# One block each for the latent stage and the relative stage of a two-layer decoder on one core

## The chip, the cores and the metric

The kernel runs on one core of a Trainium2 chip. That core has a matrix engine (TensorE, in the rows PE, with its weight loads as PEld), a vector engine (VectorE, DVE), an activation engine (ScalarE, ACT), a general engine (GpSimd, POOL), and SyncE (SP), whose queue issues the DMA transfers. The metric is the device time of one execution in microseconds, from the first to the last work of the core. Lower is better.

## What is computed

`x` has 4 batches of 512 tokens with 128 channels, all fp32. Layer 0 is an RWKV-6 block, a cross attention and a feed-forward with a dense and a sparse path. Layer 1 is a self attention with relative position tables, a cross attention of 16 heads with 64 channels on a context of 32 tokens per batch, and a guided attention in two classes. The two stages of layer 1 that the change touches are these:

```python
    def _L1_attn_ref(x, W_qkv, b_qkv, W_out, b_out, rel_emb_k, rel_emb_v):
        ...
        score = jnp.einsum('bhqd,bhkd->bhqk', q, k) + jnp.einsum('bhqd,qkd->bhqk', q, pe_k)
        attn = jax.nn.softmax(score, axis=-1)
        ctx = jnp.einsum('bhqk,bhkd->bhqd', attn, v) + jnp.einsum('bhqk,qkd->bhqd', attn, pe_v)
        ctx = jnp.transpose(ctx, (0, 2, 1, 3)).reshape(b, s, d)
        return ctx @ W_out + b_out
    def _L1_xattn_ref(latents, context, ln_l_w, ln_l_b, ln_c_w, ln_c_b, Wq, Wkv, Wo, bo):
        ...
        lat = layernorm(latents, ln_l_w, ln_l_b)
        ctx = layernorm(context, ln_c_w, ln_c_b)
        q = (lat @ Wq).reshape(b, n, H, D).transpose(0, 2, 1, 3)
        kv = ctx @ Wkv
        k, v = jnp.split(kv, 2, axis=-1)
        ...
        attn = jnp.einsum('bhnd,bhsd->bhns', q, k) * scale
        attn = jnp.clip(attn, -11.0, 11.0)
        attn = jax.nn.softmax(attn, axis=-1)
        out = jnp.einsum('bhns,bhsd->bhnd', attn, v)
        return out @ Wo + bo
    x = x + _L1_attn_ref(_layernorm(x, axis=-1), ...)
    x = x + _L1_xattn_ref(_layernorm(x, axis=-1), ctx_1024, ...)
```

## The kernel before

The stages run one after another, and each is one or more blocks. A block gives every engine its own program; between two blocks all five engines meet at a barrier. `x` stays in SBUF, channels on partitions. Engines work in the written order, and only semaphores tie them. `g.ps` is PSUM: 8 banks of 128 x 512 fp32. A matmul with a 128-row fp32 weight shows as two instructions, a transpose as one.

`norm_stage` (L138 to L178) is a layer norm in its own block: four centering matmuls (L154), four squares on ACT (L166), four mean matmuls (L158), and per batch an `Ln` and an `Exp` on ACT (L169, L172) and a product on DVE (L178).

**Relative stage.** After its norm comes a projection block (L1346 to L1448): q, k and v for four batches on PE, copies on ACT, the tables `raw` and `rel_v` and the rows `ends` by DMA (L1353, L1358, L1363), and q turned to token order (`swap`, L1396), copied by DVE into `q_tok` and stored to DRAM by SP (L1366). After the barrier the main block begins. SP first loads `qd` from that DRAM scratch (L1772); POOL builds `keys`, `qbd` (L1516) and `qrel` from `qd` (L1525); PE scores (L1552, L1562). There are 64 steps of 32 queries. In each, DVE takes four maxima (L1728), ACT four exponentials (L1695), PE turns four tiles (L1577), DVE copies two of them (L1743) and ACT two (L1684), and PE sums values near the diagonal (L1602) and far from it (L1627). DVE's `picked` (L1734, semaphore `masked`) reads the near sums, and `near_values` of the next step and the three `tail` phases of a batch wait for `masked`. At the end of each batch SP stores `o` in one transfer (L1778), waits for it, and reads it back as `ot` in eight transfers (L1786), which `tail` phase 1 (L1646, L1649) waits for. L1656 is the output product, L1763 the addition to `x`.

**Latent stage.** Two norm stages, of the tokens and of the 128 context columns, are followed by a block of weight products: K and V (L1161), their copies, A = Wq K (L1169, 16 matmuls), U = V Wo (L1178, 64 small ones), with two DVE passes for the affine part (L1199, L1202). The third block is a loop over 16 tiles of 128 tokens: score (L1239), clip in two DVE passes (L1267 from PSUM, L1271 in place), `Exp` (L1298), sum (L1253) and reciprocal (L1255), the product with it on POOL (L1281), four transposes (L1222), a copy on ACT (L1292), and per batch four output matmuls (L1232) and an addition (L1259). `p`, `total` and their PSUM banks have two buffers. PE's order in the loop is score of tile n, turn of tile n-1, and after every fourth tile all four output matmuls of a batch.

## Time and profile before

| | |
|---|---|
| median of 3 runs | 1489.88 us (1484.61 to 1497.74) |
| the profiled execution | 1488.59 us, span of its core 1486.9 us |
| PE busy | 1159.3 us, 78% of the span |
| DVE, ACT, POOL busy | 839.2 (56%), 712.7 (48%), 306.2 us (21%) |
| DMA | 51.61 MB, mean 35 GB/s |
| mean granted PE clock | 0.906 |
| relative stage with its norm | 611 to 1080.4 us |
| latent stage | 1080.4 to 1183 us |

No engine is busy all through, and the chain that ended last reaches back only to the last stage. Since stages are parted by barriers, each is read by itself: when its first and last instructions run, and which wait sets its pace. A line in a timeline merges neighbouring instructions of one kind (x4 is four of them), and the bracket behind it holds the idle time of its engine before it and what ended that.

### The profile page before, as it was taken

The page shows a single profiled execution, that of the slowest core. Times are in us where ns is not written, and L with a number is a line of the kernel's source. Part 1 is how long each engine was busy: PE and PEld are TensorE (multiplying, and loading weights), DVE is VectorE, ACT ScalarE, POOL GpSimd, SP SyncE. Part 2 cuts the span into 40 slices and gives each one's busy share as a digit, 9 for nine tenths or more (in the row PEclk, how much of TensorE's full clock was granted, in tenths as well). Part 3 has the DMA queues.
Part 4 walks back from the last instruction along what each step waited for, and adds up shares of the span by engine and source line. Part 5 has one row for each costly group of instructions (what it writes and reads, how often), then busy time and mean ns, then how long its engine had stood idle before and what let it go on. Part 6 is the DMA issues. An engine that isn't in the chain of part 4 may idle for free. (4 is left out here: it accounts for less than half of the span.)

```text
span 1486.9 us, 35646 instructions
## 1 busy us (share of the span) xinstructions
PE 1159.3 (78%) x14780; PEld 578.3 (39%) x14780; DVE 839.2 (56%) x1359; ACT 712.7 (48%) x1328; POOL 306.2 (21%) x639
## 2 busy tenths in 40 slices
PE   5677677888858997578999999999676655588886
PEld 2222332333233442246666666666443223122221
DVE  3575336777632323237666666666226342799994
ACT  4100443777522223536665665555232332389894
POOL 1443010333202322034223223222002101100000
PEclk9999866999968998689999999999889886699998
DMA  4000006111005320140030030110200000611100
GB/s 163 1 0 0 1 0 213 46 46 46 3 0 115 70 44 0 72 72 4 3 24 4 3 24 3 10 11 3 17 1 0 0 1 1 214 36 47 36 24 30
DMA packets 133665, 51.61 MB, mean 35 GB/s; under 512 B 103113, under 2 KB 125657, under 8 KB 132858
## 3 DMA queue, kind: packets, MB, share of 16 engines
q1 hardware_dynamic: 133506, 49.34, 14.3%
q8 instruction: 118, 1.93, 0.5%
q14 instruction: 41, 0.34, 0.1%
HBM read 33.12 MB, written 15.81 MB: 33 GB/s over the span
## 5 line engine op out<-in xcount | busy, mean ns | idle before, releaser
L1728 DVE TENSOR_REDUCE re_nmax<-ps 128x1 f32<-128x512 f32 x256 | 158.9, 683 | 113.1 <-PE ps L1562 113.1
L1577 PE MATMUL ps<-const,re_p 128*128 128x128 f32 x1024 | 154.8, 284 | 33.0 <-DVE re_pT L1743 26.6
L1695 ACT ACTIVATE re_p<-ps,re_nmax 128x512 f32<-128x512 f32 x256 | 154.5, 693 | 16.2 <-DVE re_nmax L1728 16.2
L850 DVE TENSOR_REDUCE ga_nmax<-ps 128x2 f32<-128x1024 f32 x128 | 147.9, 1217 | 14.3 <-PE ps L656 14.2
L1684 ACT ACTIVATE re_pT<-ps 128x512 f32<-128x512 f32 x128 | 76.6, 598 | 162.0 <-PE ps L1577 162.0
L783 ACT ACTIVATE ga_pt<-ps 128x512 f32<-128x512 f32 x256 | 139.2, 598 | 30.6 <-PE ps L691 28.9
L1577 PEld LDWEIGHTS ps<-const,re_p 128*128 128x128 f32 x1024 | 109.1, 142 | 63.4 <-ACT re_p L1695 47.2
L850 DVE TENSOR_REDUCE da_nmax<-ps 128x2 f32<-128x256 f32 (+3 forms) x128 | 102.3, 822 | 38.3 <-PE ps L667 36.9
L783 ACT ACTIVATE da_pt<-ps 128x512 f32<-128x512 f32 (+3 forms) x256 | 97.5, 438 | 46.6 <-PE ps L691 45.6
L1743 DVE COPY re_pT<-ps 128x512 f32<-128x512 f32 x128 | 82.6, 686 | 22.9 <-PE ps L1577 22.2
L710 PE MATMUL ps<-ga_pt,ga_v 128*9 128x256 f32 x1024 | 81.1, 385 | 9.6 <-ACT ga_osum L796 9.4
L1083 DVE TENSOR_TENSOR ex_u<-ps,ex_s 128x512 f32<-128x512 f32 x48 | 33.2, 692 | 96.6 <-PE ps L1056 96.6
L163 ACT ACT_TABLE_LOAD x8 | 10.3, 1283 | 153.2 <-PEq L298 91.7
L1552 PE MATMUL ps<-re_keys,re_qbd 32*128 32x512 f32 x512 | 74.9, 655 | 5.0 <-POOL re_qbd L1516 5.0
L617 POOL TENSOR_SCALAR_AFFINE_SELECT da_pt<-da_pt 128x256 f32<-128x256 f32 x128 | 52.6, 411 | 126.5 <-ACT da_pt L783 126.5
L1069 ACT ACTIVATE ex_s<-ps 128x512 f32<-128x512 f32 x48 | 28.7, 597 | 93.5 <-PE ps L1056 93.5
L1525 POOL TENSOR_TENSOR re_qrel<-re_qd,const 128x64 f32<-128x64 f32 x256 | 68.6, 300 | 4.8 <-DMA re_qd<-re_q_scratch 4.8
L1512 POOL TENSOR_TENSOR re_keys<-re_k,vec 128x64 f32<-128x64 f32 (+1 forms) x60 | 17.3, 288 | 249.7 <-PE ps L1562 249.7
L1096 POOL TENSOR_TENSOR ex_u<-ex_u,ex_gates 128x512 f32<-128x512 f32 x32 | 40.5, 1265 | 134.1 <-DVE ex_u L1083 70.5
L1627 PE MATMUL ps<-re_pT,re_v_far 128*9 128x128 f32 x1536 | 65.4, 286 | 0.5 <-ACT re_osum L1704 0.5
L656 PE MATMUL ps<-ga_kst,ga_qst 50*128 50x512 bf16 x256 | 52.9, 413 | 12.5 <-DVE ga_nmax L850 9.8
L1056 PE MATMUL ps<-ff_xn,weights 128*128 128x512 f32 x128 | 60.2, 592 | 0.0
(384 smaller groups left out, 2020.9 us busy)
## 6 DMA issues: line engine op xcount, KB each, us to landing
ex_gates<-gates_scratch SPq DMA_DIRECT2D x4, 2048.0 KB, 14.7
da_stacks<-da_qkparts SPq DMA_DIRECT2D x8, 384.0 KB, 3.1
da_qst<-da_stacks SPq DMA_DIRECT2D x32, 96.0 KB, 2.3
da_kst<-da_stacks SPq DMA_DIRECT2D x32, 96.0 KB, 2.4
ga_stacks<-ga_qkparts SPq DMA_DIRECT2D x8, 384.0 KB, 3.1
ga_qst<-ga_stacks SPq DMA_DIRECT2D x32, 96.0 KB
ga_kst<-ga_stacks SPq DMA_DIRECT2D x32, 96.0 KB
da_stacks<-da_qkparts SPq DMA_DIRECT2D x8, 256.0 KB, 3.1
```

Source lines behind the costliest of these rows:

```text
L710: last = nc.tensor.matmul(g.ps[32 * j:32 * j + HD + 1, O_BANK, lo:hi], v9[:, QT * b + kt, 4 * quad + j, :], pt[:, (4 * u + kt) % SLOTS, j, ...
L783: nc.scalar.activation(pt[:, (4 * u + kt) % SLOTS, 2 * pr + par, q0:T], g.ps[:, ST_BANK + (2 * t + par) % ST_BANKS, q0:T], ACT.Exp)\
L850: nc.vector.tensor_reduce(nmax[:, u % 2, :, pr, qt], g.ps[:, score_bank[step]:score_bank[step] + 2, 0:keys_of(qt)], AX.X, ALU.max, negate= ...
L1056: last = nc.tensor.matmul(g.ps[:, 2 * m + n % 2, :], g.w(w)[:, bass.ts(f, 128)], x[:, b, :], start=True, stop=True).then_inc(up, 1)
L1525: nc.gpsimd.tensor_tensor(qrel[:, m, pair, :, :, :, two], qd[:, b % 2, OCT * at:OCT * at + OCT, 4 * pair:4 * pair + 4].unsqueeze(2) .broad ...
L1552: nc.tensor.matmul(g.ps[:, S_BANK + quad, :], qbd[rows, m, :, :, :].rearrange("p o h c -> p (o h c)"), keys[rows, b % 2, m, :], start=True ...
L1577: last = nc.tensor.transpose(g.ps[:, T_BANK + tile % 2, bass.ts(kt, 128)], p[:, QUAD_ORDER[idx], bass.ts(kt, 128)], g.c("ident"))
L1627: last = nc.tensor.matmul(g.ps[32 * j:32 * j + HD + 1, V_BANK, bass.ts(quad, 128)], values, weights, start=kt == 0, stop=kt == QT - 1)
L1684: nc.scalar.activation(pT_of(s, QUAD_ORDER[idx]), turned_of(4 * s + idx), ACT.Identity)\
L1695: nc.scalar.activation(p[:, quad, :], g.ps[:, S_BANK + quad, :], ACT.Exp, bias=nmax[:, s % 2, idx:idx + 1]).then_inc(exped, 1)
L1728: nc.vector.tensor_reduce(nmax[:, s % 2, idx:idx + 1], g.ps[:, S_BANK + quad, :], AX.X, ALU.max, negate=True).then_inc(maxed, 1)
L1743: nc.vector.tensor_copy(pT_of(s, QUAD_ORDER[idx]), turned_of(4 * s + idx))\
```

## The change

In the latent stage the two norms, the weight products and the loop become one block. The context's norm runs in PSUM bank 4 among the token norm's instructions, with its affine part in the scaling; the K and V products follow the four mean matmuls. The additive part of the token norm goes to POOL. The factor 1/8 moves into the copy of A, so that the clip is one DVE pass. `p` and `total` have four buffers; PE turns tile n-2 after the score of tile n and makes one output matmul per tile, seven tiles behind.

```diff
+    NP = 4
+    CN, SC, TU, OUT = 4, 0, 2, 4
+    TURN_LAG, OUT_LAG = 2, 3
...
+                nc.tensor.matmul(g.ps[:, CN, 0:B * LC], g.c("center"), g.ctxT[:, :], start=True, stop=True)\
+                    .then_inc(c_centered, 1)
+                for b in range(B):
+                    nc.tensor.matmul(g.ps[:, b, :], g.c("center"), g.x[:, bass.ts(b, T)], start=True, stop=True)\
+                        .then_inc(centered, 1)
+                    if b == 0:
+                        pe.wait_ge(c_squared, 1)
+                        nc.tensor.matmul(g.ps[:, CN, bass.ts(1, B * LC)], g.c("mean"), csq[:, :], start=True,
+                                         stop=True).then_inc(c_varied, 1)
+                pe.wait_ge(c_normed, 1)
+                for b in range(B):
+                    pe.wait_ge(squared, b + 1)
+                    nc.tensor.matmul(g.ps[:, B + b, :], g.c("mean"), sq[:, b, :], start=True, stop=True)\
+                        .then_inc(varied, 1)
...
+                        if c % 4 == 0:
+                            pe.wait_ge(logged, 2 * side + c // 4 + 1)
...
+                    if n % 4 == 0:
+                        pe.wait_ge(scaled, n // 4 + 1)
...
+                pe.wait_ge(a_copied, 4)
+                for n in range(NTILE + QT + OUT_LAG):
+                    if n < NTILE:
+                        score(n)
+                    if 0 <= n - TURN_LAG < NTILE:
+                        turn(n - TURN_LAG)
+                    if n >= QT + OUT_LAG:
+                        output(*divmod(n - QT - OUT_LAG, QT))
...
+                nc.scalar.activation(csq[:, :], g.ps[:, CN, bass.ts(1, B * LC)], ACT.Ln, bias=g.eps[:, :])\
+                    .then_inc(c_logged, 1)
+                act.wait_ge(c_logged, 1)
+                nc.scalar.activation(csq[:, :], csq[:, :], ACT.Exp, scale=-0.5).then_inc(c_rooted, 1)
+                for b in range(1, B):
+                    act.wait_ge(centered, b + 1)
+                    nc.scalar.activation(sq[:, b, :], g.ps[:, b, :], ACT.Square).then_inc(squared, 1)
+                for b in range(B):
+                    act.wait_ge(varied, b + 1)
+                    nc.scalar.activation(sd[:, b, :], g.ps[:, B + b, :], ACT.Ln, bias=g.eps[:, :]).then_inc(logged, 1)
...
+                                         g.ps[:, n, :].rearrange("p (i n) -> p i n", n=128), ACT.Identity,
+                                         scale=XD ** -0.5).then_inc(a_copied, 1)
...
+                for n in range(NTILE + TURN_LAG):
+                    if n < NTILE:
+                        act.wait_ge(clipped, n + 1)
+                        flat = p[:, n % NP, :, :].rearrange("p h k -> p (h k)")
+                        nc.scalar.activation(flat, flat, ACT.Exp).then_inc(exped, 1)
+                    if n >= TURN_LAG:
+                        copy(n - TURN_LAG)
...
+                    nc.vector.scalar_tensor_tensor(out=lat[:, b, :], in0=g.ps[:, b, :], scalar=g.v("ln_l_w"),
+                                                   in1=sd[:, b, :], op0=ALU.mult, op1=ALU.mult).then_inc(scaled, 1)
...
+                def clip(n):
+                    dve.wait_ge(scored, n + 1)
+                    if n >= NP:
+                        dve.wait_ge(turned, n - NP + 1)
+                    nc.vector.tensor_scalar(p[:, n % NP, :, :].rearrange("p h k -> p (h k)"), g.ps[:, SC + n % 2, :],
+                                            11.0, -11.0, ALU.min, ALU.max).then_inc(clipped, 1)
+
+                def average(n):
+                    dve.wait_ge(exped, n + 1)
+                    if n >= NP:
+                        dve.wait_ge(normed, n - NP + 1)
+                    nc.vector.tensor_reduce(total[:, n % NP, :], p[:, n % NP, :, :], AX.X, ALU.add).then_inc(totalled, 1)
+                    dve.wait_ge(totalled, n + 1)
+                    nc.vector.reciprocal(total[:, n % NP, :], total[:, n % NP, :]).then_inc(inverted, 1)
+
...
+                for n in range(NTILE + QT + OUT_LAG):
+                    if n < NTILE:
+                        clip(n)
+                    if 1 <= n <= NTILE:
+                        average(n - 1)
+                    b, at = divmod(n - OUT_LAG - QT - 1, QT)
+                    if at == QT - 1 and b >= 0:
+                        add(b)
+                add(B - 1)
...
-                    flat = p[:, n % 2, :, :].rearrange("p h k -> p (h k)")
-                    nc.vector.tensor_scalar(flat, flat, -11.0, None, ALU.max).then_inc(floored, 1)
...
+                    pool.wait_ge(scaled, b + 1)
+                    nc.gpsimd.tensor_scalar(lat[:, b, :], lat[:, b, :], g.v("ln_l_b"), None, ALU.add)\
+                        .then_inc(lat_ready, 1)
```

In the relative stage the projections and the steps become one block (the norm stays its own). `xn`, `q_tok`, `zero` and `raw` lie in the second half of `pT`, which is first written in step 4.

```diff
+        pT_all = sb("pT", [128, 2, GS * QT * OCT * QG // 2 * 2 * H])
+        pT = pT_all[:, :, :].rearrange("p g (s t o c n) -> p g s t o c n", s=GS, t=QT, o=OCT, c=QG // 2)
+        late = pT_all[:, 1, :]
+        xn = late[:, 0:B * T].rearrange("p (b t) -> p b t", b=B)
+        q_tok = late[:, B * T:2 * B * T].rearrange("p (b t c) -> p b t c", b=B, t=QT)
+        zero = late[:, 2 * B * T:2 * B * T + T]
+        raw = late[:, 2 * B * T + T:2 * B * T + T + WIN]
...
+                pe.wait_ge(g.weights_loaded[5], 16)
+                for b in range(B):
+                    project(b)
+                    swap(b)
+                pe.wait_ge(set_up, 3)
+                pe.wait_ge(q_out, B - 1)
+                nc.tensor.matmul(g.ps[:, V_BANK, :], zero[:, 0:128], zero, start=True, stop=True)\
+                    .then_inc(cleared, 1)
+                pe.wait_ge(q_out, B)
+                nc.tensor.matmul(g.ps[:, N_BANK, 0:1], g.w("aout"), g.v("b_v"), start=True, stop=True)\
+                    .then_inc(bias_made, 1)
+                pe.wait_ge(copied, 3 * B)
+                pe.wait_ge(bias_added, 1)
+                pe.wait_ge(less, 2 * OCT + 2)
...
+                out_tokens(0)
...
+                out_tokens(1)
...
+                out_tokens(2)
+                out_tokens(3)
+                dve.wait_ge(bias_made, 1)
+                nc.vector.tensor_tensor(b_made[:, :], g.ps[:, N_BANK, 0:1], g.v("b_out"), ALU.add)\
+                    .then_inc(bias_added, 1)
...
+                    if n == 1:
+                        dve.wait_ge(q_stored, 16 * B)
+                        dve.wait_ge(less, 2 * OCT + 2)
...
+                    if s < NSTEPS:
+                        free_pT(s)
+                        for idx in range(2):
+                            dve.wait_ge(turned, 4 * s + idx + 1)
+                            nc.vector.tensor_copy(pT_of(s, QUAD_ORDER[idx]), turned_of(4 * s + idx))\
+                                .then_inc(dve_pT, 1)
...
                             g.c("own_pair").unsqueeze(1).broadcast_to([128, OCT, 2 * HD]), ALU.mult)\
                             .then_inc(masked, 1)
-                    if s < NSTEPS:
-                        free_pT(s)
-                        for idx in range(2):
-                            dve.wait_ge(turned, 4 * s + idx + 1)
-                            nc.vector.tensor_copy(pT_of(s, QUAD_ORDER[idx]), turned_of(4 * s + idx))\
...
+                    sp.wait_ge(q_out, b + 1)
+                    sp.dma_start(q_dram[b * T:(b + 1) * T, :].rearrange("(t p) c -> p t c", p=128),
+                                 q_tok[:, b, :, :]).then_inc(q_stored, 16)
+                    if b < 2:
+                        sp.wait_ge(q_stored, 16 * (b + 1))
+                        load_queries(b)
...
+                for n in range(GROUPS):
+                    b, qt = divmod(n, QT)
+                    sp.wait_ge(o_done, GS * (n + 1))
+                    octets = slice(16 * qt, 16 * qt + 16)
+                    sp.dma_start(o_dram[b, octets].rearrange("a p d -> p a d"), o[:, b % 2, octets, :])\
+                        .then_inc(o_stored, 16)
+                    sp.wait_ge(o_stored, 16 * (n + 1))
+                    if qt == QT - 1 and b + 2 < B:
+                        load_queries(b + 2)
+                    if b >= 1 and qt == 0:
...
+                    rows = o_dram[b, octets].rearrange("a p d -> (a p d)")\
+                        .rearrange("(n h two d) -> two n h d", n=64, two=2, d=HD)
+                    for two in range(2):
+                        sp.dma_start(ot[64 * two:64 * two + 64, qt, :].rearrange("p (h d) -> p h d", d=HD),
+                                     rows[two]).then_inc(ot_loaded, 16)
```

First place: DVE in the latent loop, rows of before and of after from the third tile on (`la_p` is the tile of weights, `la_total` its sums).

```order
 L1267 TENSOR_SCALAR la_p<-ps 128x512
 L1271 TENSOR_SCALAR la_p<-la_p 128x512
 L1253 TENSOR_REDUCE la_total<-la_p 128x16
 L1255 RECIPROCAL la_total<-la_total 128x16
 L1267 TENSOR_SCALAR la_p<-ps 128x512
 L1271 TENSOR_SCALAR la_p<-la_p 128x512
```

```order
 L1315 TENSOR_SCALAR la_p<-ps 128x512
 L1322 TENSOR_REDUCE la_total<-la_p 128x16
 L1324 RECIPROCAL la_total<-la_total 128x16
 L1315 TENSOR_SCALAR la_p<-ps 128x512
 L1322 TENSOR_REDUCE la_total<-la_p 128x16
```

The second pass is gone, and the sum that follows a clip is that of the tile before.

Second place: PE in the latent loop, around the first output product of before, and around that of after (`la_A` is A, `const` the identity, `la_U` is U).

```order
 L1239 MATMUL ps<-la_A,la_lat 128x512
 L1222 MATMUL ps<-const,la_p 128x128 x4
 L1232 MATMUL ps<-la_pT,la_U 128x512 x4
 L1239 MATMUL ps<-la_A,la_lat 128x512
 L1222 MATMUL ps<-const,la_p 128x128 x4
```

```order
 L1211 MATMUL ps<-la_A,la_lat 128x512
 L1220 MATMUL ps<-const,la_p 128x128 x4
 L1231 MATMUL ps<-la_pT,la_U 128x512
 L1211 MATMUL ps<-la_A,la_lat 128x512
 L1220 MATMUL ps<-const,la_p 128x128 x4
 L1231 MATMUL ps<-la_pT,la_U 128x512
```

The four output matmuls no longer stand in one piece between a score and a turn.

Third place: the queue of SP in the relative stage, from the tables on, before and then after (`re_q_scratch` and `re_o_scratch` are in DRAM; `re_pT` stands for `raw` and `q_tok`).

```order
 L1353 DMA re_raw<-in_rel_k 8x136 x16
 L1358 DMA re_rel_v<-in_rel_v 128x1024
 L1358 DMA re_rel_v<-in_rel_v 128x512 x2
 L1363 DMA re_ends<-in_rel_v 128x8 x2
 L1366 DMA re_q_scratch<-re_q_tok 128x4x128 x4
...
 L1772 DMA re_qd<-re_q_scratch 64x64x8 x4
 L1778 DMA re_o_scratch<-re_o 128x64x8
 L1786 DMA re_ot<-re_o_scratch 64x16x8 x8
```

```order
 L1817 DMA re_pT<-in_rel_k 8x136 x16
 L1821 DMA re_rel_v<-in_rel_v 128x1024
 L1821 DMA re_rel_v<-in_rel_v 128x512 x2
 L1826 DMA re_ends<-in_rel_v 128x8 x2
 L1829 DMA re_q_scratch<-re_pT 128x4x128
 L1811 DMA re_qd<-re_q_scratch 64x64x8 x2
 L1829 DMA re_q_scratch<-re_pT 128x4x128
 L1811 DMA re_qd<-re_q_scratch 64x64x8 x2
 L1829 DMA re_q_scratch<-re_pT 128x4x128 x2
 L1839 DMA re_o_scratch<-re_o 128x16x8
 L1849 DMA re_ot<-re_o_scratch 64x16x8 x2
```

The first load of `qd` stands right behind the first store, and a batch's `o` goes out and comes back in quarters.

## Rows read from the trace of the kernel before

**Rows 1.** Windows: stretch, its length, busy PE, PEld, DVE, ACT, POOL, clock, DMA share, GB/s

```profile
661.50:1049.00 387.50, 352.87 (x8935) 244.24 (x8933) 257.07 (x502) 227.84 (x392) 115.23 (x375) 1.00 0.10 9
1113.00:1184.00 71.00, 43.84 (x129) 20.02 (x129) 37.05 (x68) 18.35 (x33) 16.75 (x16) 0.88 0.00 0
```

**Rows 2.** Timeline, relative stage up to its first step: start, length, engine, line

```profile
639.16 1.29 DVE L1441 TENSOR_TENSOR re_rel_v<-re_rel_v,re_ends 128x512 f32<-128x512 f32 x2 [4.59 <-DMA re_ends<-in_rel_v]
...
643.24 1.10 PE L1404 MATMUL ps<-re_zero 128*128 128x512 f32 x2
...
646.81 8.46 SPq L1772 DMA_DIRECT2D re_qd<-re_q_scratch  x4
...
654.05 1.06 POOL L1525 TENSOR_TENSOR re_qrel<-re_qd,const 128x64 f32<-128x64 f32 x4 [4.82 <-DMA re_qd<-re_q_scratch]
...
655.17 0.90 PE L1562 MATMUL ps<-re_rel_k,re_qrel 64*32 64x72 f32 x32 [3.71 <-POOL re_qrel L1525]
```

**Rows 3.** DMA issues of the relative stage: KB each, us from issue to landing

```profile
re_q_scratch<-re_q_tok SPq DMA_DIRECT2D x4, 256.0 KB, 2.4
...
re_o_scratch<-re_o SPq DMA_DIRECT2D x1, 256.0 KB, 9.2
```

**Rows 4.** Timeline, one step of the relative stage, DVE and the next near sums

```profile
706.48 0.22 DVE L1734 TENSOR_TENSOR re_picked<-ps,const 128x64 f32<-128x64 f32 x1
...
707.14 1.29 DVE L1743 COPY re_pT<-ps 128x512 f32<-128x512 f32 x2 [0.44 <-PE ps L1577]
...
710.18 2.48 DVE L1728 TENSOR_REDUCE re_nmax<-ps 128x1 f32<-128x512 f32 x4 [1.65 <-PE ps L1562]
...
711.82 0.77 PE L1602 MATMUL ps<-re_rel_v,re_pT 128*32 128x16 f32 x64
```

**Rows 5.** Timeline, end of the relative stage and first matmul behind it

```profile
1056.19 0.36 SPq L1778 DMA_DIRECT2D re_o_scratch<-re_o  x1
...
1065.41 5.49 SPq L1786 DMA_DIRECT2D re_ot<-re_o_scratch  x8
...
1072.79 1.93 PE L1646 MATMUL ps<-re_osum,const 128*32 128x512 f32 x8 [10.71 <-DMA re_ot<-re_o_scratch]
...
1081.53 5.67 PE L154 MATMUL ps<-x,const 128*128 128x512 f32 x8 [1.94 <-PEq L109]
```

**Rows 6.** Timeline, latent stage from its first norm's last Exp to the loop

```profile
1092.52 0.63 ACT L172 ACTIVATE laln_sd<-laln_sd 128x512 f32<-128x512 f32 x1
...
1101.73 0.60 ACT L1188 ACTIVATE la_kT<-ps 128x512 f32<-128x512 f32 x1 [3.99 <-PE ps L1161]
...
1104.80 3.50 PE L1169 MATMUL ps<-la_kT,weights 64*128 64x128 f32 x32
...
1108.23 3.70 PE L1178 MATMUL ps<-weights,la_vT 64*32 64x128 f32 x128
...
1113.00 1.96 PE L1239 MATMUL ps<-la_A,la_lat 128*128 128x512 f32 x4 [1.08 <-PEq L1152]
```

**Rows 7.** Timeline, latent loop: a batch's output product, then one tile; last addition

```profile
1130.94 3.60 PE L1232 MATMUL ps<-la_pT,la_U 128*128 128x512 f32 x8
...
1134.37 1.02 PE L1239 MATMUL ps<-la_A,la_lat 128*128 128x512 f32 x2
...
1135.23 0.60 PE L1222 MATMUL ps<-const,la_p 128*128 128x128 f32 x4
...
1135.43 0.69 DVE L1267 TENSOR_SCALAR la_p<-ps 128x512 f32<-128x512 f32 x1 [3.09 <-PE ps L1239]
...
1137.28 0.69 DVE L1253 TENSOR_REDUCE la_total<-la_p 128x16 f32<-128x512 f32 x1 [0.69 <-ACT la_p L1298]
...
1138.33 1.05 POOL L1281 TENSOR_TENSOR la_p<-la_p,la_total 128x512 f32<-128x512 f32 x1 [4.86 <-DVE la_total L1255]
...
1139.44 0.66 PE L1222 MATMUL ps<-const,la_p 128*128 128x128 f32 x4 [2.74 <-POOL la_p L1281]
...
1182.18 0.75 DVE L1259 SCALAR_TENSOR_TENSOR x<-ps,vec,x 128x512 f32<-128x512 f32 x1 [9.34 <-PE ps L1232]
```

401 lines of the change are left out of this document (170 added, 231 removed).

## The prediction, made before the changed kernel ran

> **What bounds the kernel now.** The table of windows comes first [rows 1]. The 64 steps of the relative stage keep PE busy for 353 of 387.5 us at clock 1.00 (2.4 GHz). The latent loop keeps it busy for 43.8 of 71.0 us at 0.88, and DVE for 37.1: nothing is full there, so a chain of waits sets its pace. Barriers part the stages, so the timeline is read at four places: the head of the relative stage [rows 2], one step [rows 4], its end [rows 5], and the latent stage [rows 6, 7]. The reader should see POOL wait for `qd` until 654.05, PE wait 10.71 us for `ot` at the end, and POOL, PE and DVE of the latent loop each idle 2.7 to 4.9 us in a tile.
>
> **Relative stage, head.** Before, `qd` is issued at 646.81, behind a barrier; `qrel` starts at 654.05 (7.24 later) and L1562 at 655.17 (1.12 later) [rows 2]. After, the load stands behind the first store, which stands behind the tables in the same queue. The last table lands at 639.16 [rows 2]. The store takes 2.4 alone [rows 3]. If it starts only when the tables are in, it is in at 641.6; I take 640.4, since its bytes can follow theirs before the last table's receipt is back. Then L1562 starts at 640.4 + 7.24 + 1.12 = 648.8, **6.4 us earlier**; the late bound gives 5.2. Is anything else later? PE does the same matmuls in another order and ended them at 643.24 + 1.10 = 644.3 [rows 2]. It must now also wait for the last `q_tok` copy and the bias, some 0.5 us, and for the table differences (done by 640.5). So it is ready near 645, before `qd`, but an earlier store could not give more than 9. That the first step may run at a better clock is not counted.
>
> **Relative stage, steps.** `picked` moves behind the two copies. Now it fills DVE's gap: after it DVE still waits 0.44 before the copies, for PE [rows 4]. So moving it lets no copy start earlier. It ends at 707.14 + 1.29 + 0.22 = 708.65. Queued behind it are the small sum and the next maxima, which start at 710.18 after 1.65 idle: they keep over 1.2. PE's next near sums start at 711.82 [rows 4], 3.2 later. A plain step costs nothing. The `tail` phases of the first three batches wait for `masked` right after the third turn; nine such places by up to 0.25 give **1.5 lost**, bounds 0 and 2.5. The quarter stores and loads in mid-stage have four steps of 6.15 (387.5 / 63 [rows 1]) to land in and nobody waits.
>
> **Relative stage, end.** The last store of 256 KB is issued at 1056.19 and takes 9.2 to land [rows 3, 5]; the store of `q_tok`, as many bytes in long rows, takes 2.4 [rows 3], so the many short rows cost. Then come eight loads, 5.49 of issue, and 1.9 until L1646 starts at 1072.79 [rows 5]. After, a quarter is left. An equal share of 9.2 is 2.3; with a fixed part I take 4.0. Two loads issue in 5.49 / 4 = 1.4, and 1.9 more to land: 1056.2 + 4.0 + 1.4 + 1.9 = 1063.5, **9.3 earlier**. PE's own work ends at about 1062, so 10 is the most; if the quarter takes the whole 9.2, 4.1 are left. The page "DMA: Bandwidth & Descriptors" of the Trainium skill (Rules for kernel authors) says that small transfers should be joined, since below 64 KB one pays mostly overhead. A quarter has 64 KB, so by that rule splitting would win little beyond the loads' 4.1; no run here shows it yet.
>
> PE also idles 1.5 instead of 10.7 there. The norm behind it took 5.67 for eight matmuls of 128x512 [rows 5], where the same eight take 3.60 in the loop [rows 7]: it began at the low clock. If PE stays at the high one, the norm gains 2.1, and the chain from L1646 to the norm's first matmul (8.74 long, about 5 of it matmuls; 1072.79 to 1081.53 [rows 5]) gains half of that, 2.5; the row has 1.93 of it, the other products behind it are put at a like length. I take 2.4 for the chain, whose gap is short, and **1.0** for the norm, which follows more waiting: 3.4, bounds 0 and 5.
>
> **Latent stage, head.** The second norm, the affine passes and two barriers leave the path. After: PE starts as at 1081.53; the two context matmuls, a quarter as wide as those of 5.67 / 4 [rows 5], add 0.7 ahead of the mean matmuls; the context's Ln and Exp lie among the squares. The last token Exp ended at 1092.52 + 0.63 = 1093.15 [rows 6] and now ends at 1093.8. K and V run beside it, since PE has nothing else after the mean matmuls. The two K copies (0.60 each [rows 6]) stand behind that Exp in ACT's queue: 1095.0. Then A takes 1108.23 - 1104.80 = 3.43 and U, at the same rate, 3.5 [rows 6], and the first score starts at 1102.0, against 1113.00: **11.0 earlier**, bounds 10 and 11.5. The additive pass on POOL is hidden: it has until 1102 for four passes of about one microsecond (its product of that size takes 1.05 [rows 7]). If that were not so, the first score alone would wait.
>
> **Latent loop.** Work per tile at the high clock: PE has a score (0.86, from 1134.37 to 1135.23), a turn (about 0.43) and an output matmul (3.43 / 4 = 0.86, from 1130.94 to 1134.37), so 2.15; DVE has a clip (0.69), a sum (0.69), a reciprocal (under 0.3) and a quarter of an addition (0.75), 1.8; ACT an Exp and a copy, 1.23 [rows 6]; POOL 1.05 [rows 7]. But PE can turn a tile only when its chain is through. Score of tile n-1 to its clip is 1.06 (1134.37 to 1135.43); the clip holds DVE for 0.72; behind it, in order, comes the sum of tile n-2, 1.05 to POOL's start (1137.28 to 1138.33), and 1.11 to the turn (1139.44). So turn n-2 starts 3.94 after score n-1. After the turn PE has 1.29 more to the next score. Two scores are then 3.94 + 1.29 = 5.23 apart where the chain binds, a period of **2.61**, above PE's 2.15. Without output matmuls it is 2.18.
>
> Worked through from score 0 at time 0: turn 0 at 4.8, turn 1 at 6.4, then 9.1, 10.8; scores 6, 7, 8 at 11.2, 13.9, 16.4; seven more periods put score 15 at 34.8; turn 14 at 38.8 and turn 15 at 40.0; the outputs end at 45.6 and the last addition at 46.6. Before, it ran from 1113.00 to 1182.18 + 0.75, 69.9 [rows 6, 7]. The loop gives **23.3**. Bounds: 29 if PE's 2.15 sets the pace, and 18 if DVE adds 0.5 to each period.
>
> **Sum.** 6.4 - 1.5 + 9.3 + 3.4 + 11.0 + 23.3 = 51.9. The profiled execution took 1488.59 us, its span was 1486.9 with 1.7 around it, and it gives 1436.7. The median of the runs is 1.3 higher, so I forecast 1438.
>
> **Rivals.**
> A: PE is the bound in the loop, because the chain is shorter than its pieces. For it: ACT and POOL are idle more than half. Against it: DVE's order, with the next clip ahead of each sum. It gives 1438 - 5.5 = 1432.
> B: the clock. The loop before, with PE 62% busy, had 0.88 [rows 1]; if PE stays at 1.2 GHz through the new one, a tile has 4.3 of PE work instead of 2.61, 16 x 1.7 = 27 more, and the 3.4 of clock are lost: 1468. Against it: PE will be over 80% busy, and the dense steps have 1.00 [rows 1]. The page "TensorE: Matmul & The Clock Gate" of the Trainium skill (HAM oscillation) tells of kernels whose waits between groups of matmuls bring the low clock back each time; by it the fill, where PE waits 1 to 2 us per tile, is the danger.
> C: the transfers do not get shorter. Quarter store as long as the whole (5.2 less) and `qd` at its late bound (1.2 less): 1444.
> D, the other side: `picked` comes too late. Near sums wait for it in all 64 steps. It has 3.2 of room [rows 4]; each step must lose 0.8 for the gain to vanish, so it decides from a `picked` that is 4.0 later than I place it, and at 4.5 the kernel takes 1438 + 64 x 1.3 = 1521. Nothing in rows 4 speaks for that.
>
> **How the numbers follow.** Forecast 0.70, A 0.10, B 0.06, C 0.09, D 0.02, something unseen 0.03, in equal parts of gain and loss. The terms at their bad bounds give 1455, at their good ones 1423. The range 1422 to 1453 takes in A and C, and leaves out B, D and some of the rest. About 1% is what a measurement of this kernel can tell from no change, 15 us; all cases but D and half of the unseen lie beyond it on the fast side: faster 0.96, same 0.02, slower 0.02.
>
> **What would show it.** In the changed profile: the first `qrel` starts about 8.5 us after the table differences begin, not 14.9 [rows 2]; the steps still take 6.15; L1646's successor waits about 1.5 for `ot`, not 10.7; from the latent stage's first matmul to its first score 20.5 instead of 31.5; scores 2.6 apart, with PE waiting before each turn for POOL; and 46.6 from first score to last addition. The forecast is wrong if the clock of that window is below 0.9, if PE does not wait before turns (A), or if a step is longer than 6.2.

## The result, and the profile after

| | before | after |
|---|---|---|
| median | 1489.29 us (4 runs, 1484.61 to 1497.74) | 1433.13 us (4 runs, 1430.54 to 1437.26) |
| ratio, 95% interval | | 0.9619 (0.957 to 0.9668) |
| the profiled execution | 1488.59 us, span 1486.9 | 1430.54 us, span 1428.8 |
| mean granted PE clock | 0.906 | 0.925 |
| PE busy | 1159.3 us | 1142.9 us |

The forecast was 1438 us, range 1422 to 1453. In a second comparison (experiment 9) after took 1441.69 us, ratio 0.9677 (0.9652 to 0.9702); both medians lie in the range, 5 us below and 4 above the forecast. The executions with the lower time have the higher granted clock, as is shown below (experiments 9 to 11).

The two profiled executions, cut at the same places of the program:

| stretch | before | after | gain | forecast |
|---|---|---|---|---|
| start to the relative norm's first matmul (code untouched) | 613.02 | 609.68 | 3.34 | 0 |
| to the first near scores (L1562, now L1554) | 42.15 | 33.53 | 8.62 | 6.4 |
| to the last near scores, 64 steps | 393.80 | 395.01 | -1.21 | -1.5 |
| to the last tail's product with `ot` (L1646, now L1638) | 23.82 | 14.44 | 9.38 | 9.3 |
| to the latent stage's first matmul | 8.74 | 5.86 | 2.88 | 2.4 |
| to its first score | 31.47 | 19.74 | 11.73 | 11.0 + 1.0 |
| to the next norm's first matmul | 70.93 | 47.48 | 23.45 | 23.3 |
| the rest (untouched) | 302.97 | 303.06 | -0.09 | 0 |
| span | 1486.9 | 1428.8 | 58.1 | 51.9 |

The stretches that the change touches gave 54.9, where 51.9 were forecast; 3.3 more came from code that nobody touched.

The windows of after, with the columns of [rows 1]: the steps, and the loop from its first score to its last addition.

```profile
661.50:1037.20 375.70, 342.47 (x8722) 238.99 (x8714) 251.33 (x485) 220.50 (x379) 112.08 (x363) 1.00 0.12 10
1078.30:1124.70 46.40, 37.66 (x132) 16.90 (x128) 27.47 (x53) 18.63 (x32) 16.75 (x16) 1.00 0.00 0
```

The steps look as before. The loop's clock is 1.00 where it was 0.88, and PE is busy for 81% of it.

**Relative head.** Timeline of after (answers to [rows 2]): the first store of `q_tok`, the DVE sum that waits for the last table, the first load of `qd`, the first `qrel`, the first near scores.

```profile
631.17 0.43 SPq L1829 DMA_DIRECT2D re_q_scratch<-re_pT  x1
634.61 1.29 DVE L1746 TENSOR_TENSOR re_rel_v<-re_rel_v,re_ends 128x512 f32<-128x512 f32 x2 [0.95 <-DMA re_ends<-in_rel_v]
...
634.91 3.30 SPq L1811 DMA_DIRECT2D re_qd<-re_q_scratch  x2
...
642.08 1.07 POOL L1476 TENSOR_TENSOR re_qrel<-re_qd,const 128x64 f32<-128x64 f32 x4 [11.91 <-DMA re_qd<-re_q_scratch]
...
643.21 0.57 PE L1554 MATMUL ps<-re_rel_k,re_qrel 64*32 64x72 f32 x32 [0.66 <-POOL re_qrel L1476]
```

From the load's issue to `qrel` 7.17, and 1.13 more to the scores: as in the kernel before (7.24 and 1.12). `qrel` starts 7.5 behind the table sum (634.61); the forecast said 8.5, and it was 14.9 before. What was off is when the tables and the store are in: the table sum starts 11.4 behind the block's first matmul (623.23), 12.6 in the kernel before, and the store, issued ahead of the tables' landing, is in 0.3 behind the start of that sum, 3.74 after its own issue.

**Relative end.** Timeline of after (answers to [rows 5]):

```profile
1045.41 0.36 SPq L1839 DMA_DIRECT2D re_o_scratch<-re_o  x1
...
1049.59 1.23 SPq L1849 DMA_DIRECT2D re_ot<-re_o_scratch  x2
...
1052.66 1.06 PE L1638 MATMUL ps<-re_osum,const 128*32 128x512 f32 x8 [1.41 <-DMA re_ot<-re_o_scratch]
```

The last store of 64 KB takes 4.18 instead of 9.22, two loads to the product 3.07 instead of 7.38. PE waits 1.41 for `ot`, not 10.71, and L1638 runs at the high level of the clock (1.06; 1.93 in [rows 5]).

**Latent head.** Timeline of after (answers to [rows 6]): the first of the norm's mean matmuls, POOL's affine passes, K and V, the K copies, A, U, the first score.

```profile
1064.06 3.60 PE L1171 MATMUL ps<-la_sq,const 128*128 128x512 f32 x8
...
1067.36 6.22 POOL L1345 TENSOR_SCALAR la_lat<-la_lat,vec 128x512 f32<-128x512 f32 x4 [38.87 <-DVE la_lat L1300]
1067.49 3.73 PE L1180 MATMUL ps<-la_cn,weights 128*128 128x128 f32 x32
...
1070.09 1.07 ACT L1266 ACTIVATE la_kT<-ps 128x512 f32<-128x512 f32 x2
...
1071.21 3.50 PE L1190 MATMUL ps<-la_kT,weights 64*128 64x128 f32 x32
...
1074.64 3.70 PE L1199 MATMUL ps<-weights,la_vT 64*32 64x128 f32 x128
...
1078.26 1.13 PE L1211 MATMUL ps<-la_A,la_lat 128*128 128x512 f32 x2
```

The order is the forecast one: the K copies behind the last token `Exp`, then A and U without a gap. POOL's passes take 1.57 each, not about one, and end at 1073.6, 4.7 before the first score.

**Latent loop.** Timeline of after in the full loop (answers to [rows 7]), and the last addition.

```profile
1095.49 0.69 DVE L1315 TENSOR_SCALAR la_p<-ps 128x512 f32<-128x512 f32 x1 [0.70 <-PE ps L1211]
...
1095.96 0.66 PE L1220 MATMUL ps<-const,la_p 128*128 128x128 f32 x4 [0.52 <-POOL la_p L1349]
...
1097.32 1.02 PE L1211 MATMUL ps<-la_A,la_lat 128*128 128x512 f32 x2
...
1099.59 1.02 PE L1211 MATMUL ps<-la_A,la_lat 128*128 128x512 f32 x2
...
1100.02 1.05 POOL L1349 TENSOR_TENSOR la_p<-la_p,la_total 128x512 f32<-128x512 f32 x1 [1.84 <-DVE la_total L1324]
...
1101.12 0.66 PE L1220 MATMUL ps<-const,la_p 128*128 128x128 f32 x4 [0.51 <-POOL la_p L1349]
...
1102.48 1.02 PE L1211 MATMUL ps<-la_A,la_lat 128*128 128x512 f32 x2
...
1123.91 0.75 DVE L1328 SCALAR_TENSOR_TENSOR x<-ps,vec,x 128x512 f32<-128x512 f32 x1 [2.68 <-PE ps L1231]
```

Scores are 2.27 and 2.89 apart in turn, 2.58 on average. Every second turn waits 0.5 for POOL's product; the sign that the prediction gave was a wait before each turn. From first score to last addition it takes 46.4.

### The profile page after: what moved, and what is told of

The parts are those of the page before. It is cut to its first block and busy times, and to the rows that moved or that the text cites. A ratio compares the mean times of both kernels' runs of the same rounds, so it can differ in the third digit from the quotient of the medians.

```text
span 1428.8 us, 35604 instructions
## 1 busy us (share of the span) xinstructions
PE 1142.9 (80%) x14780; PEld 572.1 (40%) x14780; DVE 830.3 (58%) x1339; ACT 712.1 (50%) x1327; POOL 312.4 (22%) x643
## 3 DMA queue, kind: packets, MB, share of 16 engines
q8 instruction: 118, 1.93, 0.6%
## 5 line engine op out<-in xcount | busy, mean ns | idle before, releaser
L1569 PEld LDWEIGHTS ps<-const,re_p 128*128 128x128 f32 x1024 | 109.2, 141 | 63.9 <-ACT re_p L1706 47.5
```

The source lines that it names most:

```text
L1569: last = nc.tensor.transpose(g.ps[:, T_BANK + tile % 2, bass.ts(kt, 128)], p[:, QUAD_ORDER[idx], bass.ts(kt, 128)], g.c("ident"))
```

## The experiments

Each number of a stage below is read from the kernel's own trace, between the cut places of the table above. Medians are of 4 runs (5 in experiments 9 and 11, one run in 12). Experiments 1 to 4, 5 to 8 and 9 to 12 were three comparisons, each on one chip of its own beside the kernel before, whose medians there are 1490.4, 1492.0 and 1487.95 us.

### 1 and 2. One stage at a time

Edit 1: `relative_stage` of before with the new `latent_stage`. Edit 2: the reverse.

> The new latent stage with the relative stage of before. Theory (the gains add up): the traces of before and after differ by 11.7 us from the latent stage's first matmul to its first score and by 23.5 us from there to the next norm; so 1489.3 - 35.2 = 1454. The chain from the relative stage's last products to the latent norm keeps its 8.7 us and the low clock. Rival (coupled by the clock): part of the head's 11.7 us came from PE being at the high clock when the norm began; then the head gains about 10 only, and the time is near 1456 to 1457.

> The new relative stage with the latent stage of before. Theory: its head gives 8.6 us, the steps take 1.2 back, the end gives 9.35, the chain to the latent norm 2.9, and the old norm's eight matmuls begin at the high clock (up to 2 more): 1489.3 - 19.7 = 1470, or 1468 with those 2. Rival: the 3.3 us that the profiled execution of after gained ahead of the relative stage, in code that was not touched, belong to the change (the stage's new buffers or its placing); then 3.3 less, 1465 to 1466, and the first matmul of the relative norm stands near 609.7 in this trace too, not near 613.

Measured: latent alone 1457.87 us (1454.56 to 1461.19; ratio 0.9764, 0.9722 to 0.9806), relative alone 1470.63 us (1468.09 to 1471.45; 0.9854, 0.9821 to 0.9887).

With the latent stage alone, the head took 20.35, so 11.1 less than before, and the loop with its drain 47.51; the chain ahead kept its 8.60. That lies between theory (11.7) and rival (10), but it can't decide between them: in the eight traces where the chain ahead took 5.9 to 6.1, the same head took 19.6 to 21.2, and behind the slow chain of experiment 4 it took 19.5. The rest of the program, untouched, took 310.5 instead of 303.0 in the profiled execution (1461.2 us, the longest of the four), which accounts for its distance from the expected 1454. The windows show where, in this kernel (columns of [rows 1]):

```profile
1209.00:1239.00 30.00, 24.50 (x91) 17.07 (x91) 12.97 (x31) 12.40 (x22) 8.06 (x4) 0.66 0.15 53
```

And the same stretch of the program in after:

```profile
1185.70:1215.70 30.00, 22.57 (x103) 14.23 (x102) 16.77 (x37) 16.51 (x31) 8.04 (x4) 0.90 0.20 67
```

It is the third 30 us behind the latent stage: one execution has a clock of 0.66 there, the other 0.90, and most of the 7.5 us arise in it.

With the relative stage alone: head 34.88 (7.3 gained), steps 395.5, end 14.41 (9.4 gained), chain 7.51 (1.2 gained, not 2.9). The untouched stretch ahead took 612.03, nearer to 613.0 than to 609.7, which speaks against the rival that the new buffers gave the 3.3 us; experiments 9 to 11 settle it. The medians gained 32.5 and 19.8, together 52.3; the whole change gained 56.2 in its first comparison and 46.3 in experiment 9, so nothing says that the two parts help each other.

### 3. Two buffers instead of four

```diff
-    NP = 4
+    NP = 2
```

> After, with two buffers for the probabilities of a tile instead of four, all else as it is. Theory: the clip of tile n must wait for the turn of tile n-2, which itself is behind POOL's product; clip, Exp, sum, reciprocal, product and turn (0.73 + 0.71 + 0.71 + 0.34 + 1.10 + 0.79 from their rows, one clip of waiting besides) then go round once for two tiles, so worked through by the in-order queues the scores come 3.6 apart instead of 2.58, and the first score to the last addition takes 64 instead of 46.4: 1433.1 + 17 = 1450. Rival: four buffers matter little, since only two tiles are under way at a time and the one-pass clip and the parted output matmuls made the loop fast: period at most 2.9, under 1438.

Measured: 1457.75 us (1451.1 to 1463.09). In the trace scores are 3.52 apart, and first score to next norm takes 63.9 instead of 47.5: 16.4 lost, 17 expected. Its timeline shows a score early in the loop and, later, the new wait, the clip's for the turn two tiles back:

```profile
1090.13 1.92 PE L1211 MATMUL ps<-la_A,la_lat 128*128 128x512 f32 x2
...
1109.70 1.05 POOL L1349 TENSOR_TENSOR la_p<-la_p,la_total 128x512 f32<-128x512 f32 x1 [2.47 <-DVE la_total L1324]
1110.80 0.66 PE L1220 MATMUL ps<-const,la_p 128*128 128x128 f32 x4 [1.14 <-POOL la_p L1349]
...
1111.57 0.69 DVE L1315 TENSOR_SCALAR la_p<-ps 128x512 f32<-128x512 f32 x1 [1.95 <-PE ps L1220]
...
1113.22 1.05 POOL L1349 TENSOR_TENSOR la_p<-la_p,la_total 128x512 f32<-128x512 f32 x1 [2.47 <-DVE la_total L1324]
```

With the other edits in place, the four buffers are worth 16 of the loop's 23 us. PE ran at the low level of the clock early in the loop (1.92 for a score at 1090.13, 1.02 from 1093.7 on). The median lies 8 above the expectation; the profiled execution, the shortest of the four, took 1451.1, and the other three, at clocks 0.910 to 0.914 against its 0.922, 1455 to 1463.

### 4. Wider lags: is it a chain or PE that sets the pace?

```diff
-    TURN_LAG, OUT_LAG = 2, 3
+    TURN_LAG, OUT_LAG = 3, 4
```

> After, with a tile turned three places behind its score instead of two, and its outputs four places behind the turns' batch instead of three. Theory of the prediction (a chain sets the pace, not PE): the chain from a score through clip, the sum of the tile before and POOL's product no longer ends at PE's next turn, so PE's own pieces set the pace (0.87 + 0.49 + 0.87 = 2.2): scores 2.25 apart instead of 2.58, first score to last addition 39.5 to 41 instead of 46.4 (the drain is one tile longer, the period shorter), total 1433.1 - 6 = 1427. PE's waits before its turns are gone. Rival A (PE and its hand-offs set the pace already): period stays near 2.6 and the time at 1433.

Measured: 1429.68 us (1428.32 to 1433.61; ratio 0.9587, 0.9553 to 0.9621). First score to next norm 39.00 instead of 47.48; first score to last addition 37.9, where 39.5 to 41 were expected. Timeline of its full loop, PE's matmuls alone:

```profile
1096.17 1.02 PE L1211 MATMUL ps<-la_A,la_lat 128*128 128x512 f32 x2
1097.03 0.60 PE L1220 MATMUL ps<-const,la_p 128*128 128x128 f32 x4
1097.47 1.02 PE L1231 MATMUL ps<-la_pT,la_U 128*128 128x512 f32 x2
1098.33 1.02 PE L1211 MATMUL ps<-la_A,la_lat 128*128 128x512 f32 x2
```

And its window from first score to last addition:

```profile
1082.90:1120.80 37.90, 36.05 (x132) 17.57 (x128) 26.91 (x53) 18.30 (x32) 16.71 (x16) 1.00 0.00 0
```

A period is 2.16 and PE hardly idles: 36.1 of 37.9 us busy. This is the 2.15 that the prediction summed for PE's own pieces, 0.86 + 0.43 + 0.86. So in after the chain set the pace, as forecast, and rival A falls. The bracket of every second turn said so already; the proof is that the period moves when only the lag is changed.

### 5. `picked` back ahead of the copies

```diff
-                    if s < NSTEPS:
-                        free_pT(s)
-                        for idx in range(2):
-                            dve.wait_ge(turned, 4 * s + idx + 1)
-                            nc.vector.tensor_copy(pT_of(s, QUAD_ORDER[idx]), turned_of(4 * s + idx))\
-                                .then_inc(dve_pT, 1)
...
                             .then_inc(masked, 1)
+                    if s < NSTEPS:
+                        free_pT(s)
+                        for idx in range(2):
+                            dve.wait_ge(turned, 4 * s + idx + 1)
+                            nc.vector.tensor_copy(pT_of(s, QUAD_ORDER[idx]), turned_of(4 * s + idx))\
+                                .then_inc(dve_pT, 1)
```

> After, with the copy of the near sums (picked) put back ahead of the two copies of the turned tiles. Theory (the prediction's term of 1.5): first to last near scores takes 395.0 us in after and 393.8 in before, of which the first step gave 0.8 back, so the move costs about 2 over nine tail phases: here near 393, and 1433.1 - 2 = 1431. Rival (the dearer steps come from the new order of stores and loads, not from the move): first to last near scores stays at 395, and the time at 1433.

Measured: 1440.96 us (1438.75 to 1441.92), 8 above the first median of after and level with its second, where 1431 or 1433 was expected; the medians say nothing here. First to last near scores 394.8, between theory (393) and rival (395). The sum of 63 steps is a poor measure here: in ten profiled executions with `picked` behind the copies it lies between 394.5 and 397.3, since the first step takes 6.2 to 6.3 or 7.0 and single steps now and then 0.3 to 1.1 more. The steps of the `tail` show the edit. The first and the fourth of four near scores in a row, around the first tail, in after:

```profile
769.59 0.69 PE L1554 MATMUL ps<-re_rel_k,re_qrel 64*32 64x136 f32 x32
...
792.59 0.69 PE L1554 MATMUL ps<-re_rel_k,re_qrel 64*32 64x136 f32 x32
```

And in this kernel:

```profile
775.73 0.69 PE L1554 MATMUL ps<-re_rel_k,re_qrel 64*32 64x136 f32 x32
...
798.11 0.69 PE L1554 MATMUL ps<-re_rel_k,re_qrel 64*32 64x136 f32 x32
```

Three tail steps take 23.00 with `picked` behind the copies and 22.38 with it ahead (22.37 in the kernel before). Three batches have a tail among the steps: against the kernel before after loses 0.63 in each, 1.9 us; against this kernel 0.62, 0.61 and 0.41, 1.6 us. Most other steps are alike. The term of the prediction (nine places, 1.5) stands, and the rival (stores and loads make the steps dearer) falls for these steps, since the stores are the same in both kernels. Only steps show it, no median.

### 6. The whole batch in one store

```diff
-                for n in range(GROUPS):
...
-                    sp.wait_ge(o_done, GS * (n + 1))
...
+                for b in range(B):
+                    sp.wait_ge(o_done, STEPS_B * (b + 1))
+                    sp.dma_start(o_dram[b].rearrange("a p d -> p a d"), o[:, b % 2, :, :]).then_inc(o_stored, 16)
```

> After, with the output store of the relative stage as one per batch again and eight loads behind it. Theory: the last store takes 9.2 from its issue to the loads' issue instead of 4.2, the loads to the tail's first product 7.4 instead of 3.1: 9.35 later; PE then waits some 10 us, and the chain to the latent norm runs in part at the low clock, 0 to 2.9 more: 1433.1 + 9.4 to 12.3, so 1442 to 1446. Rival (the store is quick for another reason than its size, such as nothing else under way in its queue): the last store takes under 6, and the time is at most 1439.

Measured: 1450.2 us (1444.92 to 1462.54). Last near scores to the tail's product 23.69 instead of 14.44 (9.25, expected 9.35), and the chain behind it 7.65 instead of 5.86. The profiled execution took 1446.28; the median lies 4 above the expected 1442 to 1446. Its timeline:

```profile
1049.41 0.36 SPq L1837 DMA_DIRECT2D re_o_scratch<-re_o  x1
...
1058.37 5.56 SPq L1845 DMA_DIRECT2D re_ot<-re_o_scratch  x8
...
1065.87 1.94 PE L1638 MATMUL ps<-re_osum,const 128*32 128x512 f32 x8 [10.62 <-DMA re_ot<-re_o_scratch]
```

The store takes 8.96 again, so the rival falls, and PE starts again at the low level of the clock (1.94 for L1638) after waiting 10.62.

### 7. The clip in two passes again

```diff
-                                            11.0, -11.0, ALU.min, ALU.max).then_inc(clipped, 1)
+                                            11.0, None, ALU.min).then_inc(clipped, 1)
...
+                    nc.vector.tensor_scalar(flat, flat, -11.0, None, ALU.max).then_inc(floored, 1)
```

> After, with the bounding of the latent scores in two passes on DVE again (the upper bound, then the lower). Theory: DVE is part of the chain that sets the pace, and the second pass (0.73 by the row of the first) stands in it: by the in-order queues the period goes from 2.58 to 2.98, first score to last addition from 46.4 to about 53: 1433.1 + 6.4 = 1439.5. Rival: DVE is idle for a third of the loop (12 of 46 us before its clips), so the pass is hidden: under 1435.

Measured: 1446.86 us (1441.22 to 1450.49). First score to next norm 51.4, 3.9 more than after; the period is 2.81. The median is 7 above the expected 1439.5, and the untouched stretch behind took 309.8 in this trace, 6.7 more than in after. The second pass does stand in the chain, so the rival (hidden) falls, but its price was taken from the wrong row. The two passes of one tile:

```profile
1107.27 0.69 DVE L1316 TENSOR_SCALAR la_p<-ps 128x512 f32<-128x512 f32 x1 [0.45 <-PE ps L1212]
1107.99 0.43 DVE L1320 TENSOR_SCALAR la_p<-la_p 128x512 f32<-128x512 f32 x1
```

The pass that reads SBUF and writes in place takes 0.43, the one from PSUM 0.69, of the same 128x512. So the one-pass clip saves DVE 0.43 a tile against this kernel, and the period 0.23 (2.81 to 2.58). In the kernel before the same pass was dearer in seven of 16 tiles:

```profile
1120.12 1.05 POOL L1281 TENSOR_TENSOR la_p<-la_p,la_total 128x512 f32<-128x512 f32 x1 [2.03 <-DVE la_total L1255]
...
1120.62 0.83 DVE L1271 TENSOR_SCALAR la_p<-la_p 128x512 f32<-128x512 f32 x1
```

Where POOL's product had begun 0.50 earlier, the pass took 0.83 and ended 0.28 behind the product; where the product had begun 0.74 earlier, it took 0.59 and again ended 0.28 behind; with no product under way it took 0.43. That looks like a pass that is held up until POOL is done; no experiment was made on it.

### 8. The four output matmuls together

```diff
-                    if n >= QT + OUT_LAG:
-                        output(*divmod(n - QT - OUT_LAG, QT))
+                    if n >= QT + OUT_LAG and (n - QT - OUT_LAG) % QT == 0:
+                        for grp in range(QT):
+                            output((n - QT - OUT_LAG) // QT, grp)
```

> After, with the four output matmuls of a batch issued one after the other behind the fourth turn, instead of one behind each turn. Theory: three tiles of four have a period of 2.2 then, the fourth bears 3.4 of outputs more; by the queues the loop takes 2.8 longer: 1436. Rival (the spreading was needed to keep PE's chain short): the loop takes over 5 longer, with scores held up at each batch, 1438 and more. Second rival: the same time, 1433.

Measured: 1444.75 us (1441.76 to 1448.84). First score to next norm 50.2, 2.7 more than after, 2.8 expected. PE's timeline at one batch's end:

```profile
1112.76 3.60 PE L1231 MATMUL ps<-la_pT,la_U 128*128 128x512 f32 x8
...
1116.19 1.02 PE L1211 MATMUL ps<-la_A,la_lat 128*128 128x512 f32 x2
```

The first rival (over 5) falls. The second (the same time) falls by the loop; the medians could not tell 2.7, and 1444.75 is 9 above what was expected, with 308.9 for the untouched stretch behind.

### 9 to 11. After again, the wider lags, and both edits together

> After itself once more, beside the two kernels that follow, on one chip. In the profiled executions so far, code that none of the edits touch took 609.7 to 614.9 us ahead of the relative stage's norm and 303.0 to 310.5 behind the latent stage. Theory: this comes from the granted clock of the execution and not from the kernel: at mean clocks near 0.915 after takes 1437 to 1441, at 0.925 near 1431. Rival: the other kernels' untouched parts were slower because of their edits; then after repeats 1433 and 609.7 / 303.1.

> The kernel with the wider lags (three and four places) again, beside after on the same chip. Its trace showed a period of 2.16 and 39.0 from the first score to the next norm, against 47.5. Theory: it keeps these 8.5, so its median is 7 to 9 below that of after in this comparison. Rival: PE's denser work in the loop is given back as a lower clock behind it, so that only 3 to 4 are left, as in the medians so far (1433.1 and 1429.7).

> The wider lags, and the copy of the near sums back ahead of the two copies of the turned tiles. Theory (the move of that copy costs nothing that can be measured: first to last near scores took 394.8 with it ahead and 394.5 to 396.9 with it behind): within 1 us of the kernel with the wider lags alone. Rival (the prediction's term): 1.5 to 2 us faster than that.

Measured, side by side: after 1441.69 us (1434.91 to 1443.21; ratio 0.9677, 0.9652 to 0.9702); wider lags 1432.58 (1429.83 to 1436.58; 0.9625, 0.9599 to 0.965); wider lags with `picked` ahead 1429.07 (1424.4 to 1435.12; 0.9602, 0.9576 to 0.9628).

After did not repeat 1433: its median is just above what the theory of experiment 9 said (1437 to 1441 near a clock of 0.915). Each execution of after in the two comparisons, with its mean granted clock:

```
clock  0.925   0.922   0.921   0.921   0.921   0.917   0.914   0.913   0.913
us     1430.5  1433.1  1433.2  1434.9  1436.0  1437.3  1442.0  1441.7  1443.2
```

About 1 us for each 0.001 of clock, one kernel, nothing changed. The executions of the kernel before do the same (1485.3 at 0.910, 1493.7 at 0.901). The mean clock does not fix the time, though: with the wider lags, four executions at 0.917 took 1428.9 to 1433.6. The change of PE time is in places that differ from run to run: a norm in layer 0 at 142 us, here in the timeline of the kernel before:

```profile
142.31 5.94 PE L154 MATMUL ps<-rw_o,const 128*128 128x512 f32 x8 [1.21 <-PEq L298]
```

And in that of after:

```profile
141.80 3.67 PE L154 MATMUL ps<-rw_o,const 128*128 128x512 f32 x8 [1.20 <-PEq L298]
```

The same eight matmuls take 5.94 or 3.67. The untouched stretches took between 609.7 and 615.0 us ahead and 303.0 to 310.5 behind in the fourteen profiled executions. That this is not the edits' doing is shown by the kernel with the wider lags, which was traced twice: 610.7 ahead and 304.7 behind in experiment 4, 615.0 and 308.9 in experiment 10. So the 3.3 us of the table are no part of the change. Behind the latent stage the clock accounts for the spread: 303.0 to 303.2 at 0.88 in the kernel before and in both traces of after, 308.9 at 0.85 in experiments 8 and 10. Ahead it does so only in part: at 0.89 the stretch took 613.0 in the kernel before, 610.7 in experiment 4 and 614.9 in experiment 8. What decides the clock in an execution stays open.

The wider lags keep all of their 8.5 us in the trace (38.99), and the medians differ by 9.1 here; at a clock of 0.917 the one execution of after took 1437.3, and the four with the wider lags took 1428.9 to 1433.6 (1429.8 and 1430.1 in this comparison). The rival, that the gain is given back as clock, said 3 to 4 and falls. That only 3 to 4 us lay between the first medians fits the clocks there: 0.917 to 0.925 in the executions of after, 0.914 to 0.917 in those of the wider lags.

Putting `picked` ahead as well gave 3.5 us less again in the median, with overlapping intervals (their clocks are 0.912 to 0.921 and 0.910 to 0.917). My expectation of no difference was drawn from the sum over all steps; the tail steps of experiment 5 say 1.6 to 1.9, which is the rival's figure; the medians alone would not show it. This last kernel has the lowest median of all, 12.6 us under that of after beside it.

### 12. Half stores, and the sum ahead of the clip

```diff
-                for n in range(GROUPS):
+                for n in range(GROUPS // 2):
...
+                    if 1 <= n <= NTILE:
+                        average(n - 1)
                     if n < NTILE:
                         clip(n)
-                    if 1 <= n <= NTILE:
-                        average(n - 1)
```

> After with two edits in two stages, each read in its own stretch of the trace. First, the relative stage's outputs are stored by halves of a batch (128 KB) with four loads behind each. Theory (a fixed part of 2.5 us and 1.67 for each 64 KB, the line through 64 KB in 4.2 and 256 KB in 9.2): the last store takes 5.9. Rival (time in proportion to the bytes, 9.2 / 2, with 64 KB at a floor): 4.6. Second, in the latent loop DVE takes the sum of tile n-1 ahead of the clip of tile n. Theory: turn and product come earlier, but the next clip now waits for Exp and sum, so the chain clip, Exp, sum, reciprocal (0.73 + 0.71 + 0.71 + 0.26 = 2.41) sets the pace, and the drain is longer: period 2.4, first score to last addition 46.5 to 47.5, no gain. Rival (only the order of clip and sum kept the loop from PE's pace): period 2.16 to 2.2, and under 43.

Measured: 1446.46 us in one run. The last half store:

```profile
1051.91 0.36 SPq L1839 DMA_DIRECT2D re_o_scratch<-re_o  x1
...
1057.92 2.64 SPq L1850 DMA_DIRECT2D re_ot<-re_o_scratch  x4
```

6.01 for 128 KB: the line with a fixed part holds (5.9), the rival (4.6) falls. So the last store of 64, 128 and 256 KB of this layout takes 4.18, 6.01 and 8.88 to 9.22 (64 KB between 3.07 and 4.61 over ten traces, 128 KB in one trace). The loop with the sum first, one tile:

```profile
1113.47 0.63 DVE L1315 TENSOR_SCALAR la_p<-ps 128x512 f32<-128x512 f32 x1
...
1114.13 0.63 ACT L1287 ACTIVATE la_p<-la_p 128x512 f32<-128x512 f32 x1 [1.10 <-DVE la_p L1315]
...
1114.80 0.69 DVE L1322 TENSOR_REDUCE la_total<-la_p 128x16 f32<-128x512 f32 x1 [0.70 <-ACT la_p L1287]
...
1115.52 0.25 DVE L1324 RECIPROCAL la_total<-la_total 128x16 f32<-128x16 f32 x1
1115.69 0.63 DVE L1315 TENSOR_SCALAR la_p<-ps 128x512 f32<-128x512 f32 x1
```

The period is 2.21, and first score to last addition 44.5. The ring that the theory named is there and binds: clip to `Exp` 0.66, to the sum 0.67, to the reciprocal 0.72, to the next clip 0.17, together 2.22. Its price of 2.41 was too high in three of the four pieces, and so the loop won 2 us where none was expected. Neither theory nor rival hit: the ring's 2.22 lies only 0.06 above PE's own 2.16, but first score to last addition is 6.6 longer than the 37.9 of the wider lags. Most of that arises early. The fourth score stands 5.2 behind the first instead of 2.9, since PE turns a tile after the third score and not after the fourth; the next five come 2.2 apart and once 3.1, where with the wider lags and the clip ahead most follow after 1.4, and that makes 3.8 more.

## Why the prediction held, step by step

**Relative head, 6.4, measured 8.6 (7.2 to 8.9 over all kernels with the new stage).** The load, `qrel` and the scores stand where they were put behind the load's issue. The step that was mis-sized is "I take 640.4", which put the store's landing 13.9 us behind the block's first matmul (626.54 then); the load was issued 11.7 behind it (634.91 against 623.23) in after and 13.05 in experiment 2. Of the 2.2 us in after, 1.2 are the tables', whose last one was in at 11.4 instead of 12.6; the rest is the store, in 0.3 behind it instead of 1.2. From the store's issue to the load's issue it took 3.7 to 3.9 us in four traces and 5.0 to 5.3 in the other eight with the new stage; which of the two comes, and why, stays open. In the short case PE is nearly late itself: it waits only 0.66 for `qrel`, so that the "9" which the prediction gave as the most was about right.

**`picked`, -1.5, measured -1.9 in the tail steps**, hidden in the plain steps as argued. The first step takes 6.2 to 6.3 or 7.0 instead of 7.11, which was not counted. The prediction's step of 6.15 is a slip: its window of 387.5 us holds 62 steps, not 63. Without the first step, the mean is 6.24 before and 6.27 after, so "longer than 6.2" could not serve as a sign.

**Relative end, 9.3, measured 9.4.** Store 4.0, found 4.18; loads 3.3, found 3.07. The page "DMA: Bandwidth & Descriptors" of the Trainium skill (Rules for kernel authors) warned that below 64 KB mostly overhead is paid. The runs agree on the overhead: the line through 4.18 and 9.22 has a fixed part near 2.5 us (an estimate), more than half of a quarter's 4.18, and the 6.01 of 128 KB lies 0.15 above it. The figure is rough: with the 3.07 or the 4.61 of other traces in place of 4.18 it is 1.0 or 3.1. They do not agree that splitting wins little here, because three of the four quarter stores lie under the steps and only the last is waited for.

**Clock, 3.4, measured 2.9 in the chain; the norm's 1.0 is not shown.** In after the norm again starts at the low level: its first two centering matmuls took 1.91, and all eight 4.9 instead of 5.67. The head as a whole varies by 1.6 from trace to trace (19.5 to 21.2, one and the same code), and not with the chain ahead of it, so that neither 1.0 nor the 0.6 between after and experiment 1 can be told apart from that. The chain's 2.9 hold for after and are not sure for every execution: of the ten traces with quarter stores, the chain took 5.85 to 5.87 in seven, 6.11 in one and 7.5 in two. The wait for `ot` does not tell them apart: after 1.80 us of it L1638 took 1.92 in experiment 4, after 1.82 it took 1.07 in experiment 9.

**Latent head, 11.0 and 1.0 for the clock, measured 11.7 in all, and 11.1 in experiment 1, ahead of which the chain was as slow as before.** Every item stood in the forecast order. POOL's pass was put at one microsecond and took 1.57; nothing waited for it.

**Latent loop, 23.3, measured 23.5.** The period was worked out as half of 3.94 + 1.29 and measured as 2.58 against 2.61, with the bound named (POOL's product ahead of a turn) and confirmed by the one edit that takes it away (experiment 4). In the rows the two parts are 3.80 (score at 1097.32 to turn at 1101.12) and 1.36 (to the score at 1102.48), so two small errors cancel in part. What each edit is worth with the others in place: four buffers 16.4, outputs one by one 2.7, one-pass clip 3.9.

**Rivals.** A (PE's pace) was wrong for this kernel and its number, 2.15 a tile, was right for the one with wider lags. B (low clock in the loop) did not come: the new loop had 1.00 in every kernel but the one with two buffers (0.95). The page "TensorE: Matmul & The Clock Gate" of the Trainium skill (HAM oscillation) tells of waits between groups of matmuls that bring the low clock back. In after it did not come back: neither in the fill, with waits of 1.7, 1.4 and 1.4 us ahead of turns, nor in the full loop with 0.5. With two buffers it did, and in the fill, as the rival had it, behind waits of 1.7 and 1.2 us; later in that loop waits of 2.0 and then 1.1 us in each tile left the clock at 1.00. C (transfers not shorter) and D (`picked` too late) did not come.

**How much the total says.** The terms missed by +2.2, +0.1, +0.5, -0.3 and +0.2 (relative head, its end, chain, latent head, loop) and the steps by +0.3, and 3.3 us came from outside the change. That the two medians lie on both sides of the forecast is in part luck: after alone took 1430.5 to 1443.2 with nothing changed. The stretches are the evidence, not the total. The good end of the range was summed too wide as well: the prediction's own good bounds (9, 0, 10, 5, 11.5 and 29) give 1425, not 1423.
